# A mixture-of-experts and attention kernel: six shared-expert tiles moved behind the others, the routing tables made beside them, and two programs joined into one

## The reference, cut to what matters

```python
xn = layernorm(x)                                    # mean, variance over the 512
# gated branch, on xn
gates = softmax(xn @ router_w.T)                     # 8 experts
topv, topi = top_k(gates, 2)                         # normalised to sum 1
routed = sum over experts e of gate_e * ((silu(xn @ wg_e) * (xn @ wu_e)) @ wd_e)
shared = (silu(xn @ sg) * (xn @ su)) @ sd            # hidden 704 = 2 x 352
g = silu(routed + shared)
# attention branch, on xn, layer-normalised again
n = layernorm(xn) * gamma + beta
s = softmax(causal(q k^T / sqrt(512))) @ v @ o_proj + xn
out = xn + s * g
```

## Time and profile before

| | |
|---|---|
| median of 3 runs | 1262.59 us |
| the profiled execution | 1259.98 us, its span 1258.2 us |
| TensorE busy, share of the span | 1176.6 us, 94% |
| VectorE, ScalarE, GpSimd busy | 598.5, 456.3, 343.9 us |
| stage 0 | 0 to 47 us |
| stage 1 and 2 | 47 to 446 us |
| stage 3 | 446 to about 860 us |
| stage 4 | from there to 1258 us |

### The profile page before, as it was taken

How to read it: one execution, slowest core, us unless ns; L and a number is a source line. 1 busy time by engine, 2 the same in 40 slices (tenths; PEclk the granted TensorE clock), 3 DMA queues, 4 the chain that set the end, 5 groups by cost and what they waited for, 6 DMA issues and landing times. The chain is left out here.

```text
span 1258.2 us, 21972 instructions
## 1 busy us (share of the span) xinstructions
PE 1176.6 (94%) x6958; PEld 653.6 (52%) x6959; DVE 598.5 (48%) x1198; ACT 456.3 (36%) x822; POOL 343.9 (27%) x430
## 2 busy tenths in 40 slices
PE   5899999999999559999999999997899999999996
PEld 3455555556565235555555555553444444454443
DVE  5555555555555831112112211225765776776455
ACT  4433333333332112222222222223553553554452
POOL 1030000000001431212221221212554564565653
PEclk9899999999999769999999999998999999999999
DMA  8567666766674149977777777765268368257364
GB/s 298 165 161 188 168 165 179 192 166 164 178 187 107 44 92 255 218 188 174 175 183 178 174 179 179 174 153 174 76 151 225 92 149 237 85 123 204 106 146 109
DMA packets 324802, 206.44 MB, mean 164 GB/s; under 512 B 263168, under 2 KB 271368, under 8 KB 324368
## 3 DMA queue, kind: packets, MB, share of 16 engines
q1 hardware_dynamic: 313920, 170.39, 54.1%
q0 software_dynamic: 10800, 35.40, 10.8%
q10 hardware_dynamic: 32, 0.02, 0.0%
HBM read 96.88 MB, written 45.88 MB: 113 GB/s over the span
## 5 line engine op out<-in xcount | busy, mean ns | idle before, releaser
L444 PE MATMUL pair<-arena 128*128 (+1 forms) x3240 | 509.6, 314 | 13.1 <-DMA arena<-arena 13.1
L444 PEld LDWEIGHTS pair<-arena 128*128 128x128 f16 x3240 | 316.2, 98 | 193.0 <-issue 15.0
L451 PE MATMUL bank<-arena 128*128 (+1 forms) x1215 | 289.9, 385 | 8.9 <-ACT arena L884 5.1
L451 PEld LDWEIGHTS bank<-arena 128*128 128x128 f16 x1215 | 119.9, 99 | 138.8 <-issue 13.1
L1265 DVE SCALAR_TENSOR_TENSOR arena<-pair,arena 128x352 f32<-128x352 f32 x71 | 37.2, 525 | 269.9 <-ACT arena L1237 266.1
L1517 PE MATMUL pair<-arena 128*128 128x512 f16 x672 | 154.1, 385 | 2.9 <-PEq L1122 2.9
L1237 ACT ACTIVATE arena<-pair 128x352 f32<-128x352 f32 x71 | 33.0, 464 | 214.5 <-PE pair L444 214.5
L1517 PEld LDWEIGHTS pair<-arena 128*128 128x128 f16 x672 | 66.6, 99 | 78.9 <-issue 7.4
L1545 PE MATMUL bank<-arena 128*128 128x512 f16 x432 | 98.6, 379 | 7.9 <-DMA arena<-arena 7.9
L201 POOL TENSOR_TENSOR root_seed<-var_eps,minus_half 128x1 f32<-128x1 f32 x32 | 17.6, 551 | 318.6 <-DVE var_eps L210 318.5
L1532 PE MATMUL pair<-arena 128*128 128x512 f16 (+3 forms) x576 | 98.9, 326 | 1.1 <-ACT arena L1589 1.1
(11 more groups left out here) (164 smaller groups left out, 1162.0 us busy)
## 6 DMA issues: line engine op xcount, KB each, us to landing
arena<-in_L_attn_x_dram SPq DMA_DIRECT2D x96, 256.0 KB, 3.4
slot_rows<-arena SPq DMA_DIRECT2D x71, 256.0 KB
xn_rows<-arena SPq DMA_DIRECT2D x32, 256.0 KB, 2.4
shared_rows<-arena SPq DMA_DIRECT2D x32, 256.0 KB, 2.6
arena<-shared_rows SPq DMA_DIRECT2D x32, 256.0 KB, 2.9
out_dram<-arena SPq DMA_DIRECT2D x32, 256.0 KB, 3.3
arena<-in_L_ffn_wg_dram SPq DMA_DIRECT2D x32, 176.0 KB, 3.0
arena<-in_L_ffn_wu_dram SPq DMA_DIRECT2D x32, 176.0 KB, 3.4
```

The costliest lines, as they stand in the source:

```text
L444: last = pe.matmul(bank[:, 0:H], xt[:, a, c, :], weights(c, b, col), start=(c == 0 and i == 0), stop=(c == KC - 1 and i == 2))
L451: last = pe.matmul(bank[:, :], ht[:, a, c, :], weights(c, b), start=(start and c == 0 and i == 0), stop=(stop and c == HC - 1 and i == 2))
```

## The change

Six tiles, 5, 9, 13, 17, 21 and 25, are normalised, routed and stored in their order as before, but their shared units wait until all other tiles' units are done. Stage 1 becomes 32 written-out **steps**: steps 0 to 25 do the units of the 26 other tiles, steps 26 to 31 those of the six.

- Steps 3, 6, 9, 12, 15 and 18 normalise two tiles instead of one, and the steps after them turn and route two. There are three buffers for turned tiles (`xt`) instead of two. Two router banks alternate.
- The low part of x goes from VectorE to GpSimd (`x_low`).
- The 32 gate-and-up chunks are spread over 18 of the first 24 steps (those that normalise one tile): 14 of these take two chunks, four take one. The second chunk of a step is split after the step's second silu and hidden. One down chunk goes to each of the steps 0 to 23, through one staging buffer instead of two, before the second silu.
- A deferred tile is turned again for its late step, by a DMA transpose that reads `xn_rows` in DRAM (`turn_late`).
- The routing runs beside steps 24 to 29, a piece after each unit of VectorE's queue. GpSimd's product with the token numbers is gone; VectorE makes each of the 64 tile tables by one `tensor_scalar` of 71 columns with two per-partition scalars.
- Stage 1, 2 and 3 are one Block (`expert_stages`). The first gathers are issued when the tokens are named, the first slot's gate_up stands behind the last tile's, and the slots' buffers are those of stage 1.

```diff
+        DEFERRED = (5, 9, 13, 17, 21, 25)
+        USUAL = [n for n in range(NT) if n not in DEFERRED]
+        LATE = len(USUAL)
...
+            def routed_in(s):
+                return range(USUAL[s] + 1, USUAL[s + 1] + 1) if s + 1 < LATE else ()
+            def normal_in(s):
+                return routed_in(s + 1)
...
+            SPLIT_STEPS = LATE - 2
+            FULL = [s for s in range(SPLIT_STEPS) if len(normal_in(s)) < 2]
+            def in_chunks(s):
+                if s not in FULL:
+                    return ()
+                i, n = FULL.index(s), len(FULL)
+                return range(i * E * KC // n, (i + 1) * E * KC // n)
+            def down_chunks(s):
+                return (s,) if s < E * HC else ()
...
-                v.tensor_tensor(hot_tile[n % RING], column[:].unsqueeze(1).to_broadcast([P, TG, W]),
-                                slot_hi[:, c, tiles].unsqueeze(2).to_broadcast([P, TG, W]), ALU.is_equal
-                                ).then_inc(in_tile_ready, 1)
+                for i in range(TG):
+                    t = first + i
+                    v.tensor_scalar(hot_tile[n % RING][:, i, :], column[:], slot_hi[:, c, t:t + 1], token_mid[:, t:t + 1],
+                                    ALU.is_equal, ALU.mult).then_inc(hot_ready, 1)
...
+            ROUTING = LATE - 2
+            def routing(dve, s, b):
+                at = 2 * (s - ROUTING) + b
+                if at == 1:
+                    pick_best(dve, 0)
...
+                elif at == 6:
+                    one_hot(dve, 0)
+                    one_hot(dve, 1)
...
+                elif at == 11:
+                    name_experts(dve)
+                    name_tokens(dve)
...
+                    def turn_late(s):
+                        d = s - LATE
+                        t = DEFERRED[d]
+                        sp.wait_ge(xn_stored[t % 2], (t // 2 + 1) * 16)
+                        sp.wait_ge(gu_done, 2 * s - 2)
+                        sp.dma_start_transpose(xt[d % 2].rearrange("p s c t -> p (s c) t"), xn_rows[t * P:(t + 1) * P, :]
+                                               ).then_inc(late_turned[d % 2], 16)
+                    def load_weights(s):
+                        for i in in_chunks(s):
+                            u, e, r = i % 2, i // KC, i % KC
+                            wait(sp, in_lo, i - 1)
...
+                    for s in range(NT):
+                        for t in routed_in(s):
+                            if t > 1:
+                                turn_x(t)
+                                store_x16(sp, t)
+                        if s + 1 >= LATE and s + 1 < NT:
+                            turn_late(s + 1)
+                        if s == NT - 1:
+                            turn_slot_x(0)
+                        if s > 0:
+                            turn_h(2 * s - 1)
+                        if s > 1:
+                            store_y(s - 2)
+                        load_weights(s + 1)
+                        turn_h(2 * s)
+                        load_down(s + 1)
+                        for t in normal_in(s):
+                            if t + 2 < NT and t + 2 > 3:
+                                load_x(t + 2)
+                    turn_slot_x(1)
+                    turn_h(2 * NT - 1)
...
+                    def x_low(t):
+                        u = t % 2
+                        pool.wait_ge(x16_hi, t + 1)
+                        pool.tensor_tensor(x16[u][:, 1], xb[u], x16[u][:, 0], ALU.subtract).then_inc(x16_lo, 1)
+                        pool.wait_ge(x16_lo, t + 1)
...
+                    for j in range(2):
+                        slot_in(j, j, 0)
+                        unit_down(2 * NT - 2 + j, j)
...
+                    for s in range(NT):
+                        silu(2 * s, 0)
+                        for i in in_chunks(s)[:1]:
+                            in_high(i)
+                        h_high(2 * s, 0)
...
+                        for t in normal_in(s):
+                            x_high(t)
+                        for i in down_chunks(s):
+                            down_high(i)
+                        silu(2 * s + 1, 1)
...
+                        for i in in_chunks(s)[1:]:
+                            in_high(i)
+                        h_high(2 * s + 1, 1)
+                        if s > 0:
+                            y_copy(s - 1)
...
-        stages1and2()
-        stage3()
+        expert_stages()
         stage4()
```

More of the change, by code:

```diff
@@ L1110, in early, with over_slots @@
+            slot_y_stored = slot_rows_stored
             def early(j, n):
                 return isinstance(j, int) and j < n
-            def over_slots(eng, tile, peeled, done=0):
-                for j in range(done, peeled):
-                    tile(j, j % 2, j // 2, False)
-                with eng.Fori(peeled // 2, (T - 1) // 2) as i:
+            def over_slots(eng, tile, first):
+                with eng.Fori(first // 2, (T - 1) // 2) as i:
                     tile(2 * i, 0, i, False)
@@ L1181, in _, with router @@
                 @block.tensor
                 def _(pe):
+                    def router(t):
+                        pe.wait_ge(x_turned[t % 3], (t // 3 + 1) * 16)
+                        wait(pe, logits_kept, t - 1)
+                        for c in range(KC):
+                            for i, (a, b) in enumerate(PARTS):
+                                last = pe.matmul(logit_bank[t % 2][:, 0:E], xt[t % 3][:, a, c, :],
+                                                 rw_split[:, c, b, :],
+                                                 start=(c == 0 and i == 0), stop=(c == KC - 1 and i == 2))
+                        last.then_inc(logits_done, 1)
@@ new lines, in hot_product @@
+                    def hot_product(n):
+                        pe.wait_ge(lane_ready, n + 1)
+                        pe.wait_ge(hot_ready, (n + 1) * TG)
+                        for t in range(TG):
+                            last = pe.matmul(token_bank[:, 0:W], hot_lane[n % RING][:, t, :], hot_tile[n % RING][:, t, :],
+                                             start=(n == 0 and t == 0), stop=(n == 2 * PARTS_HOT - 1 and t == TG - 1),
+                                             skip_group_check=True)
+                        last.then_inc(hot_used, 1)
@@ new lines, in silu, with h_high @@
+                    def silu(n, b):
+                        act.wait_ge(gu_done, n + 1)
+                        wait(act, h_lo, n - 1)
+                        nc.scalar.activation(sbuf[b], g_banks[b][:, 0:H], ACT.Silu,
+                                             scale=UNIT_SCALE).then_inc(silu_done, 1)
+                    def h_high(n, b):
+                        act.wait_ge(h_ready, n + 1)
+                        wait(act, h_turned[1 - b], (n // 2 + b) * 16)
+                        nc.scalar.copy(h_parts[:, 0, 0:H], sbuf[b]).then_inc(h_hi, 1)
```

1102 lines of the change are left out of this document (531 added, 571 removed).

## The result

The changed kernel takes 1272.25 us (median of 5 runs, 1267.45 to 1278.85) against 1262.11 (5 runs of the kernel before in the same comparison, 1260.27 to 1263.6): ratio 1.0101, 95% interval 1.0075 to 1.0127. It is slower by 10 us where 1244 was forecast; 1224 to 1256 missed it. The profiled execution took 1267.45 us, the fastest of the five; its span is 1265.7, against 1258.2 before, so the trace shows 7.5 us of the 10.

What follows compares the result with a forecast made beforehand. TensorE was taken to bound stage 1 and the slots, with a hole at the seam between them. 1259.98 - 37.4 + 13.4 + 4.8 + 0.4 = 1241.2 us; the median, 2.6 above, gave 1244, range 1224 to 1256.

Steps and rivals of the forecast that it cites:

- The seam: Between stage 1's last units and the first slots: TensorE's hole and low clock go, saving 37.4 us.
- stage 1 stays fed: Rival: stage 1's added waits shrink towards 0, giving 1225.6 us; chance 0.25 for 1224 to 1236.
- The tables: Routing tables made on VectorE beside TensorE: TensorE waits once or twice at a table product, 0.4 us.
- (a): Stage 1 steps taking two chunks: the first unit's transpose lands late, TensorE waits before its down in seven steps, 13.4 us.
- (b): Six stage 1 steps with two tiles: the second turn of x lands late for its router product, 0.8 us each, 4.8.
- (c): Stage 1 items costed at nothing: low part on GpSimd, turns from DRAM, written-out steps, the exponentials' table loads.
- Full clock all through: Sign to look for in the new profile: the granted clock never falls.
- TensorE's own waiting resets the chain: Argument against late steps in stage 1 adding up: each wait of TensorE gives the chain that much time back.
- crowded: Rival: each late stage 1 step makes the next late, 28 to 30 us in all, 1254 to 1256 us; chance 0.17.
- Slower: Rival: turns from DRAM land too late in the late steps, 1274 us at a landing of 18 us; chance 0.04.

Runs made afterwards that it cites:

- loop_cut_low: `loop_cut` with the low part of x back on VectorE: 1228.43 us, ratio 0.9747 to the kernel before.
- loop_cut_chunk: `loop_cut` with the second chunk's load again ahead of the transpose of the step's first unit: 1251.13 us, ratio 0.9926 to the kernel before.
- loop_cut: `both_orders` with next down-chunk and x loads behind the turn, turn_h between a double step's two turns, stores last: 1233.08 us, ratio 0.9789 to the kernel before.
- both_orders: The changed kernel with the edits of `chunk_order` and `router_apart` together: 1260.82 us, ratio 1.0035 to the kernel before.
- chunk_order: The changed kernel with the second chunk's load moved behind the transpose of the step's first unit: 1267.21 us, ratio 1.0069 to the kernel before.
- router_apart: The changed kernel with a double step's second router product moved behind the step's second unit: 1270.95 us, ratio 1.0115 to the kernel before.
- y_first: The changed kernel with ACT's y_copy ahead of h_high in seven steps: 1271.78 us, ratio 1.0097 to the kernel before.
- loop_together: `loop_cut` with both router products of a double step together again ahead of its first unit: 1230.39 us, ratio 0.9761 to the kernel before.
- turn_h_between: `chunk_order` with turn_h between a double step's two turns of x and the stores behind, loads left at the step's end: 1251.92 us, ratio 0.9939.

## Why the prediction was wrong

- **The seam, -37.4 us: right.** 37.4 by the same reckoning, no hole, full clock. `loop_cut_low` shows that the gain is real: with stage 1 fed, the kernel is at 0.9747 of the one before; the rival "stage 1 stays fed" says 1225.6 / 1262.6 = 0.9707.
- **The tables, 0.4: right.** One wait of 0.41 us, and 1.90 + 1.22 for a group against the 3.0 of the prediction.
- **(a), 13.4: size nearly right.** Waits of 1.75, 1.76, 1.76, 1.73, 1.61, 2.98 and 3.66, together 15.3, in the seven steps named. But the prediction ends each wait with the transpose's landing, and in the trace ACT's y_copy, which stands behind h_high, ends it. `loop_cut_chunk` prices the term at some 17 us with the clock in it.
- **(b), 4.8: wrong, 18.0.** Only the second product was to wait, 0.8 us each time; it waits 1.0 to 1.95, 7.7 in all. The first one, for which the prediction has no wait, waits 1.0 to 3.3 us in each of the six, 10.3 in all. The reason given for the size, the burst of DMA, is borne out in part: in the six double steps the first turn landed 3.9 to 5.6 us after its issue and the second 3.7 to 5.1, against the 3.6 of the prediction, so up to 2 us of each wait. But not for the reason of a full DMA: `loop_cut` runs at a higher share with hardly a wait. (By the prediction's own figures, 215.8 against 214.71 + 0.3, the wait is 0.8 us before any burst, not 0.7.)
- **(c), nothing: wrong for GpSimd's low part.** The text saw that it might slow VectorE beside it and put 0.4 us of that into (b). Not followed was what stands behind down_low: load_down waits for it in SyncE's queue ahead of the turn of x, 42.4 us in all; in the step shown above that wait outlasts x_low by 0.55 us (243.76 to 244.31). The Trainium skill (GPSIMD Engine Reference, Specifications) says that GpSimd's SBUF interface is shared with VectorE, with contention for VectorE's instructions with two SBUF inputs; down_low's 1315 against 683 ns agrees. How much of TensorE's waits comes of this is not shown: with the loop cut, taking x's low part off GpSimd changes nothing that can be told. Of the other parts of (c), the six turns from DRAM (issued at 382.51 to 440.44) were right: they landed in 3.3 to 3.4 us, under the 4 to 6 assumed, and never let TensorE wait.
- **The clock: left out.** The sum had its waits as bare durations. In five double steps the waits cost another 1.2 to 2.3 us of slow matmuls after them, 8.6 us, and at the last two downs of (a) 2.9, so 11.5 us in all. "Full clock all through" was the prediction's own mark, and it failed.
- **The step that failed** is that each late step was priced by itself, and the lateness taken to fade: "TensorE's own waiting resets the chain". A wait of TensorE gives that chain time only if the chain does not itself go around through SyncE. It does: in `both_orders` one turn of it takes 11.35 us, as long as TensorE's step of 11.34, and 16.2 in a double step, so lateness stayed. The order of SyncE's issues alone gave back 43 us (the moved second chunk some 17, the rest of the loop's cut some 24). The rival "crowded" had this direction at 0.17, but priced it at 28 to 30 us; it was 34.3 of waits and 11.5 of clock, and with the 1.3 us of start and table and the unplaced 1.4 that is 48.5. "Slower" came true, but not by the DRAM turns on which that rival stood.

`chunk_order`, `router_apart` and `y_first` show that removing the named waits one by one does not give their time back, and `both_orders` gives back 8 us; `loop_cut`, `loop_together` and `turn_h_between` that shortening the loop does. Not separated: how much of this is the places in the queue and how much the faster landing of the turns. Not tried: a version with the long loop and no fall of the clock, so the clock's share is read from the slow instructions and not shown by a run. Why runs of the changed kernel spread over 11 us is open too; those before spread over 3 in the same comparison, but over 10 in another (1255.39 to 1265.33).

## What to carry to other kernels

Before fusing steps or thinning them out, follow one issue queue around until it comes back to itself, and compare that loop's length with the bound engine's step: at a hundred per cent busy the profile shows no wait, and hides how little is left. In an in-order issue queue, put first what the loop needs next, and the stores and loads that nobody waits for last; that alone turned a change that lost 1% into one that gains 2.4% here. When a wait is removed and shows up elsewhere at nearly the same size, look for the loop. Do not drop the first edit for it: moving the second chunk's load gave some 4 us before the loop was cut and some 17 after.

## What the runs showed of the hardware

- The clock can fall between short waits: after idling 1.19 and 1.42 us with one router product between, TensorE took 5.42 us for 24 matmuls that take 3.74 otherwise, after 3.31 and 0.97 us it took 6.08. After 0.99 and 1.39 us it took 3.74, and the down at 156.60, after 1.76 us, took 2.10 us, as at full clock.
- A two-input operation of VectorE beside GpSimd's 1.2 us one took 1315 ns on average, alone 683.
- DMA at a share of 0.85 to 0.93, with an estimated third of its bytes in transposes (the prediction's 0.65 of 1.97 MB a tile), fed stage 1 with 3.8 us of waits; at 0.68 to 0.73 (80 to 320 us), with the long loop, TensorE waited 34.3 us in the stage.
- A turn of one tile of x landed 3.0 to 3.1 us after its issue in the kernel before, 3.5 to 5.6 in the changed one. Read from DRAM in the quiet late steps, the same turn took 3.3 to 3.4.
